# First layer's weighted sums of a two-layer graph network: lane one-hots written straight as float32r by VectorE, six of seven bins weighed by ScalarE

## What is computed

```
hi, hj = h[src], h[dst]
e = leaky_relu(concat([hi, hj]) @ w, 0.2) @ a
att = exp(e) / segment_sum(exp(e), src)[src]
out = segment_sum(hi * att, dst)
x = layernorm(x + out)
```

## Time and profile before

| | us |
|---|---|
| median of 3 runs | 3264.69 |
| lowest, highest | 3262.2, 3265.74 |
| the profiled execution: its time | 3265.05 |
| its span | 3263.3 |
| busy in the span: PE, DVE, ACT | 3041.6, 3045.0, 2752.0 |

### The profile page before, as it was taken

How to read it: one execution, slowest core, us unless ns; L and a number is a source line. 1 busy time by engine, 2 the same in 40 slices (tenths; PEclk the granted TensorE clock), 3 DMA queues, 4 the chain that set the end, 5 groups by cost and what they waited for, 6 DMA issues and landing times. The chain is left out here.

```text
span 3263.3 us, 101516 instructions
## 1 busy us (share of the span) xinstructions
PE 3041.6 (93%) x40072; PEld 2778.3 (85%) x40072; DVE 3045.0 (93%) x4921; ACT 2752.0 (84%) x6952; POOL 154.7 (5%) x251
## 2 busy tenths in 40 slices
PE   5777699999999998799999999989999999999995
PEld 4666677877777786799999999988999999999993
DVE  8999889999999999899999999989999999999996
ACT  6988788888888886899999999977888888888886
POOL 0000000000000000000000000000111111111110
PEclk9989899999999999899999999999999999999998
DMA  2000022222222222233323333324444444444431
GB/s 66 13 13 12 22 93 94 93 88 92 94 87 93 94 93 57 71 96 96 97 97 96 97 96 96 98 81 154 161 164 161 164 161 162 163 160 164 161 137 41
DMA packets 173823, 333.06 MB, mean 102 GB/s; under 512 B 54876, under 2 KB 109616, under 8 KB 173264
## 3 DMA queue, kind: packets, MB, share of 16 engines
q1 hardware_dynamic: 170996, 323.30, 30.6%
q10 hardware_dynamic: 2348, 3.20, 0.3%
HBM read 320.77 MB, written 5.66 MB: 100 GB/s over the span
## 5 line engine op out<-in xcount | busy, mean ns | idle before, releaser
L1009 PE MATMUL l_gathered<-xp,l_src_onehot 128*128 128x128 bf16 x7203 | 467.0, 221 | 11.2 <-DVE l_src_onehot L922 11.2
L1434 PE MATMUL l_gathered<-hp,l_onehot 128*128 128x128 bf16 x7203 | 458.5, 219 | 0.0
L704 PE MATMUL sc_z<-sc_onehot,pq 128*128 128x256 f32 (+1 forms) x2450 | 419.5, 293 | 23.3 <-DVE sc_leaky L617 18.3
L1009 PEld LDWEIGHTS l_gathered<-xp,l_src_onehot 128*128 128x128 bf16 x7203 | 407.9, 99 | 26.3 <-DVE l_src_onehot L922 11.7
L847 DVE TENSOR_TENSOR l_lane<-iota_b,l_lane_pairs 128x896 bf16<-128x896 bf16 x686 | 421.0, 614 | 0.0
L617 DVE SCALAR_TENSOR_TENSOR sc_leaky<-sc_z,sc_leaky 128x1024 f32<-128x1024 f32 (+3 forms) x325 | 370.1, 1139 | 53.0 <-ACT sc_leaky L788 45.7
L788 ACT ACTIVATE sc_leaky<-sc_z 128x1024 f32<-128x1024 f32 (+3 forms) x325 | 309.6, 953 | 123.6 <-PE sc_z L708 120.8
L1434 PEld LDWEIGHTS l_gathered<-hp,l_onehot 128*128 128x128 bf16 x7203 | 406.2, 98 | 0.4
L708 PE MATMUL sc_z<-sc_onehot,pq 128*128 128x256 f32 (+1 forms) x2450 | 393.8, 282 | 0.0
L1448 PE MATMUL l_acc<-e,l_lane_wide 128*128 128x132 f32 x2744 | 385.7, 283 | 0.3 <-ACT e L1512 0.3
L704 PEld LDWEIGHTS sc_z<-sc_onehot,pq 128*128 128x128 f32 x2450 | 334.4, 191 | 35.6 <-issue 34.2
(11 more groups left out here) (244 smaller groups left out, 6104.2 us busy)
## 6 DMA issues: line engine op xcount, KB each, us to landing
rows_got<-edge_rows_wide SPq DMA_DIRECT2D x338, 448.0 KB, 3.6
l_got<-edge_rows_src SPq DMA_DIRECT2D x343, 224.0 KB, 3.1
placed<-edge_rows SPq DMA_DIRECT2D x144, 512.0 KB, 3.6
out_dram<-X SPq DMA_DIRECT2D x12, 256.0 KB
S<-edge_rows_wide SPq DMA_DIRECT2D x5, 448.0 KB, 8.1
edge_rows<-e SPq DMA_DIRECT2D x98, 6.1 KB
edge_rows_wide<-e SPq DMA_DIRECT2D x98, 12.2 KB
sc_last_rows<-edge_rows SPq DMA_DIRECT2D x24, 64.0 KB, 3.4
```

The lines of the kernel that those rows point to most:

```text
L704: nc.tensor.matmul(z[:, b, 0:nw, :], PQ[:, b0 + b, q, 0:C], hot[:, r % HOTS, b, 0, 0:nw, :], start=(b == u and q == 0), stop=False)
L1009: ins = nc.tensor.matmul(gps[:, t % 2, i * P:(i + 1) * P], hot[:, t % RING, i, :], parts[:, g * GX + i, q, :], start=(q == 0), stop=(q == 2))
L1434: ins = nc.tensor.matmul(gps[:, t % 2, i * P:(i + 1) * P], dst_hot[:, t % RING, i, :], hp[:, g * GX + i, q, 0:C], start=(q == 0), stop=(q ...
```

## The change

- `find_lanes` compares the lane numbers with `k.SL` directly, each lane spread over 128 elements, and writes float32r `lane_wide` itself. There are now three buffers of it (`WIDE` = 3), and the instruction waits until tile t-3 is added up.
- `lane`, `lane_pairs`, `widen` and `stage` are gone.
- VectorE weighs one bin of a tile (the last, `LAST` = 6) with a tensor_scalar, and ScalarE the six others: `weigh_first` the four that are split, and `weigh_rest` two more, with `take_high` between them.
- take_high now waits for ScalarE's own weighing. add_up waits for weigh_rest (`messages`), for VectorE's bin (`last_message`) and for `lane_wide`.

```
@@ layer0_sums, VectorE
 def weigh(t):
     dve.wait_ge(s["gathered"], t + 1)
     if t >= 2:
-        dve.wait_ge(s["low"], t - 1)
-    nc.vector.tensor_tensor(msg[:, t % 2, 0:SPLIT], gps[:, t % 2, 0:SPLIT * P].rearrange("p (i c) -> p i c", i=SPLIT),
-                            e0[:, n, g * GX:g * GX + SPLIT].unsqueeze(2).to_broadcast([P, SPLIT, C]), ALU.mult
-                            ).then_inc(s["messages"], 1)
+        dve.wait_ge(s["added"], t - 1)
+    b = g * GX + LAST
+    nc.vector.tensor_scalar(msg[:, t % 2, LAST, :], gps[:, t % 2, LAST * P:GX * P], e0[:, n, b:b + 1], None, ALU.mult
+                            ).then_inc(s["last_message"], 1)
...
 def find_lanes(t):
-    if t >= 2:
-        dve.wait_ge(s["lane_wide"], t - 1)
-    if g == 0:
-        dve.wait_ge(s["staged"], n + 1)
-    compare_lanes(nc, k, lane[:, t % 2], lane_pairs[:, n % 2, g * GX:(g + 1) * GX, :]).then_inc(s["lane"], 1)
+    if t >= WIDE:
+        dve.wait_ge(s["added"], t - WIDE + 1)
+    nc.vector.tensor_tensor(lane_wide[:, t % WIDE], k.iota_b[:].unsqueeze(1).to_broadcast([P, GX, P]),
+                            k.SL[:, 1, n, g * GX:(g + 1) * GX].unsqueeze(2).to_broadcast([P, GX, P]), ALU.is_equal
+                            ).then_inc(s["lane_wide"], 1)
@@ TensorE
 def add_up(t):
-    pe.wait_ge(s["late_messages"], t + 1)
+    pe.wait_ge(s["messages"], t + 1)
+    pe.wait_ge(s["last_message"], t + 1)
     pe.wait_ge(s["lane_wide"], t + 1)
@@ ScalarE
-def widen(t):
-    act.wait_ge(s["lane"], t + 1)
-    if t >= 2:
-        act.wait_ge(s["added"], t - 1)
-    nc.scalar.copy(lane_wide[:, t % 2], lane[:, t % 2]).then_inc(s["lane_wide"], 1)
...
+def weigh_first(t):
+    act.wait_ge(s["gathered"], t + 1)
+    if t >= 2:
+        act.wait_ge(s["added"], t - 1)
+    weigh(t, range(SPLIT)).then_inc(s["first_messages"], 1)
+
+def weigh_rest(t):
+    act.wait_ge(s["last_message"], t + 1)
+    weigh(t, range(SPLIT, LAST)).then_inc(s["messages"], 1)
 
 def take_high(t):
-    act.wait_ge(s["messages"], t + 1)
+    act.wait_ge(s["first_messages"], t + 1)
     nc.scalar.copy(halves[:, t % 2, :, 0, :], msg[:, t % 2, 0:SPLIT]).then_inc(s["high"], 1)
...
-widen(0)
 for t in range(R):
...
-    weigh_late(t)
+    weigh_first(t)
     take_high(t)
-    if t + 1 < R:
-        widen(t + 1)
-    if t % PER == 3 and t // PER + 1 < NB:
-        stage(t // PER + 1)
+    weigh_rest(t)
```

More of the change, by code:

```diff
@@ L854, in layer0_sums @@
     R = NB * PER
-    RING, LOADS, SPLIT = 3, 4, 4
+    RING, LOADS, SPLIT, LAST, WIDE = 3, 4, 4, GX - 1, 3
     BY_SCALAR = (2, 4, 6)
@@ L866, in layer0_sums @@
             "chain", "scaled", "scaled_late", "part_high", "part_rest", "part_middle", "part_low",
-            "hot", "staged", "lane", "lane_wide", "gathered", "messages", "late_messages", "high", "low", "added", "taken", "summed", "stats")}
+            "hot", "lane_wide", "gathered", "messages", "first_messages", "last_message", "high", "low", "added", "taken", "summed", "stats")}
         loaded = [ctx.semaphore(f"l0_loaded{h}") for h in range(LOADS)]
@@ L871, in layer0_sums @@
         hot = sb("src_onehot", [P, RING, GX, P], BF16)
-        lane, lane_wide = sb("lane", [P, 2, GX, P], BF16), sb("lane_wide", [P, 2, GX, P], F32R)
-        lane_pairs = sb("lane_pairs", [P, 2, NB, 2], BF16)
+        lane_wide = sb("lane_wide", [P, WIDE, GX, P], F32R)
         msg, halves = sb("messages", [P, 2, GX, C]), sb("message_halves", [P, 2, SPLIT, 2, C], F32R)
@@ L1005, in gather @@
                         pe.wait_ge(s["messages"], t - 1)
-                        pe.wait_ge(s["late_messages"], t - 1)
+                        pe.wait_ge(s["last_message"], t - 1)
                     for i in range(GX):
@@ L1019, in add_up @@
                     for i in range(SPLIT, GX):
-                        nc.tensor.matmul(acc[:, n % 2, 0:C], lane_wide[:, t % 2, i, :].bitcast(F32), msg[:, t % 2, i, :],
+                        nc.tensor.matmul(acc[:, n % 2, 0:C], lane_wide[:, t % WIDE, i, :].bitcast(F32), msg[:, t % 2, i, :],
                                          start=(g == 0 and i == SPLIT), stop=False, skip_group_check=True)
@@ L1024, in add_up @@
                         last = g == PER - 1 and i == SPLIT - 1
-                        ins = nc.tensor.matmul(acc[:, n % 2, 0:2 * C], lane_wide[:, t % 2, i, :],
+                        ins = nc.tensor.matmul(acc[:, n % 2, 0:2 * C], lane_wide[:, t % WIDE, i, :],
                                                halves[:, t % 2, i].rearrange("p h c -> p (h c)"), start=False, stop=last,
@@ L1049, in part_middle, with weigh @@
                     nc.scalar.copy(parts[:, chunk(c), 1, :], xs[:, chunk(c), :]).then_inc(s["part_middle"], 1)
-                def widen(t):
-                    act.wait_ge(s["lane"], t + 1)
-                    if t >= 2:
-                        act.wait_ge(s["added"], t - 1)
-                    nc.scalar.copy(lane_wide[:, t % 2], lane[:, t % 2]).then_inc(s["lane_wide"], 1)
-                def weigh_late(t):
-                    n, g = divmod(t, PER)
+                def weigh(t, some):
+                    n, g = divmod(t, PER)
+                    for i in some:
+                        b = g * GX + i
+                        ins = nc.scalar.activation(msg[:, t % 2, i, :], gps[:, t % 2, i * P:(i + 1) * P], ACT.Copy,
+                                                   scale=e0[:, n, b:b + 1])
+                    return ins
+                def weigh_first(t):
                     act.wait_ge(s["gathered"], t + 1)
```

## The result

| | before | changed |
|---|---|---|
| median, us | 3264.3 (4 runs) | 3284.8 (4 runs) |
| lowest, highest | 3262.2, 3265.7 | 3284.7, 3285.8 |
| ratio, 95% interval | | 1.0062 (1.0047 to 1.0077) |
| the profiled execution's span | 3263.3 | 3283.1 |

The change makes the kernel 20.5 us slower. 3288 was forecast, in a range of 3264 to 3308.

A forecast was written before the change was run, and what follows sets the result against it. The old bound was the circle take_high, take_low, make, weigh at 2.42 us a tile; a new circle of 2.50 would replace it. From 3264.7, +27 steady, -4.5 ramp and +0.7 end gave 3288 us, range 3264 to 3308.

The forecast's parts named there:

- What bounded the kernel before: Steady tiles before: a circle of waits between ScalarE and VectorE sets 2.42 us a tile, TensorE only 0.04 behind.
- the block's extras: VectorE's L941, L946 and L950, once in 7 tiles in the old circle, 0.6 us together.
- The new circle: Gather, four bins, take_high, two bins, add_up, next gather: 5.00 us for two tiles, 2.50 a tile, +27 us.
- The alternation: Steady part: gather starts alternately 2.38 and 2.62 us apart, L1020 waiting 0.24 us once in two tiles.
- VectorE's sum hidden: VectorE's steady work with the longer compare: 2.28 us a tile, covered by TensorE's 2.38, so costing nothing.
- The 0.26 for a weighing more: ScalarE: each added bin costs 0.26 us by the L1064 row, where the skill's formula gives 0.29.
- The ramp: Start of the stage, up to gather of tile 7: shorter waits for three chunks give -4.5 us, between -6 and -1.
- The term that failed: Ramp: TensorE, at half its clock in parts, may give back some of the -5.4 us, leaving -4.5.
- The sum: Whole kernel: 27 for the steady part, -4.5 ramp, +0.7 end, +23 us in all, 3288 us.
- the circle was not short enough: Rival in the steady part: circle under 4.76 us, TensorE alone sets 2.38 a tile, 3248 us; chance 0.12.
- VectorE was not the bound: Rival in the steady part: compare over 1.22 us makes VectorE decide; at 1.5, 2.78 a tile, 3382 us; chance 0.03.
- the granted clock stayed at 1.00: Rival on TensorE's clock: a twentieth of 860 us at 1.2 GHz adds 20 us, 3308 us; chance 0.06.

The follow-up runs named there:

- Run 3: Changed kernel with ScalarE's order weigh_first, weigh_rest, take_high, so all six bins come before take_high: 3320.0 us, ratio to before 1.0166.
- Run 1: Changed kernel with add_up on TensorE summing VectorE's bin first and only then waiting for ScalarE's last two bins: 3249.8 us, ratio to before 0.9948.
- run 7: Changed kernel with ScalarE weighing all seven bins and VectorE none: 3325.1 us, ratio to before 1.0202.
- run 8: Changed kernel with VectorE weighing two bins in one tensor_tensor and ScalarE five: 3244.5 us, ratio to before 0.9940.
- run 2: Changed kernel with the compare of the lanes cut from 7 bins to 3 from the fourth tile on: 3284.1 us, ratio to before 1.0056.
- run 9: Run 1's kernel with VectorE's one bin weighed as a tensor_tensor instead of a tensor_scalar: 3247.2 us.
- run 11: Run 1's kernel and the unaltered changed kernel measured again on one chip: 3246.4 us (0.9941) and 3284.0 us (1.0054).
- run 6: Kernel before with only the new weighing (ScalarE six bins, VectorE one), bf16 compare and ScalarE's cast kept: 3482.5 us, ratio 1.0663.

## Why the prediction was right

- *What bounded the kernel before.* The circle of take_high, take_low, make and weigh at 2.34 us plus the block's extras gave 2.42. Run 3 closed the same circle once more, by another edge, and its terms added up to the measured 2.60.
- *The new circle.* Forecast 5.00 us for two tiles, measured 5.01 in the timeline and 2.50 a tile in the mean. Run 1 took a third of L1020 out of it, run 7 put a bin in and run 8 took one out, and the time moved as the sum of the circle did, until VectorE's sum was met in run 8. The alternation was there as well: in the two tiles above the gathers start 2.40 apart (1708.04 to 1710.44) and then 2.61, where 2.38 and 2.62 were forecast, and L1020 waited 171 times in the stage (forecast: about 170), for 0.18 us and not 0.24.
- *VectorE's sum hidden.* Right: the compare took 1.08 us as L904 does in the earlier trace rows, and run 2 showed that none of it is on the path. Its neighbour was mis-sized: the single bin took 0.344 us, 0.26 from start to start, where the line through the earlier trace rows gave 0.29 and 0.21. The line was right for the form that it was drawn from (0.282 in run 9), and the tensor_scalar costs 0.06 more. It didn't matter here, but it made 0.06 us a tile, 20 of the 25 us, by which the expectation of run 8 was off.
- *The 0.26 for a weighing more.* The row was right: four bins last 1.14 and two 0.62 in the changed kernel, and run 7 gives 0.26 for the seventh (5.27 - 5.01 for two tiles). By the price of the Trainium skill ("ScalarE: Activation LUTs", What ACT_TABLE_LOAD costs), 0.29 from start to start, a tile would have been 2.58 as the prediction has it, an estimate. The measurement decides for the row. By the same estimate four bins and two come to 0.18 us more than the 1.14 and 0.62 measured, where the prediction counted 0.15; that would be 2.59 a tile.
- *The ramp.* Forecast -4.5 with an end at -6, measured -6.6. The chunks went as worked out: part_rest to part_rest was 6.48, 4.30 and 6.49 us (forecast 6.4, 4.2, 6.4), in these rows of the ramp:

```profile
1308.94 1.08 DVE L909 TENSOR_TENSOR R<-R,xp 128x896 f32<-128x896 f32 x1
...
1312.31 1.08 DVE L909 TENSOR_TENSOR R<-R,xp 128x896 f32<-128x896 f32 x1
...
1318.79 1.09 DVE L909 TENSOR_TENSOR R<-R,xp 128x896 f32<-128x896 f32 x1 [1.16 <-ACT xp L1045]
...
1323.09 1.09 DVE L909 TENSOR_TENSOR R<-R,xp 128x896 f32<-128x896 f32 x1
...
1329.58 1.09 DVE L909 TENSOR_TENSOR R<-R,xp 128x896 f32<-128x896 f32 x1 [2.17 <-ACT xp L1045]
```

  From the first of these rows to the last it is 20.64 us, where before it was 25.77 (1310.40 to 1336.17): -5.1, near the -5.4 of the prediction. The term that failed is TensorE's: I let it give 0.9 us of that back. In the profiled execution it gained 1.5 us more, at the full clock in 1335 to 1340 us where the earlier trace rows has 0.75. That is partly luck. In the second profile of the changed kernel (run 11) the same three distances are 6.48, 4.31 and 6.48, but the clock was at its lower level in these 5 us, and the ramp gave 5.0 us. The two stretches, first profile and second:

```profile
1335.00:1340.00 5.00, 4.63 (x56) 4.22 (x54) 5.00 (x11) 4.14 (x14) 0.00 (x0) 1.00 0.37 88
```

```profile
1335.00:1340.00 5.00, 4.75 (x32) 4.66 (x33) 4.73 (x8) 3.30 (x9) 0.00 (x0) 0.50 0.31 82
```

- *The sum.* 27 - 4.5 + 0.7 = 23 was forecast. 26.4 - 6.6 + 0.7 = 20.5 is what the trace has for the stage. The medians differ by 20.5 too, the profiled spans by 19.8, and in run 11, on another chip, the medians by 17.8 (3284.0 and 3266.2). So the agreement to the tenth is chance; the steady part's 26.4 against 27 is what bears the forecast out.
- *The rivals.* None came: the circle was not short enough, VectorE was not the bound (run 2), and the granted clock stayed at 1.00 in 1500 to 1700 us with TensorE waiting 0.18 us every other tile.

## What to carry to other kernels

Sum each engine's work for a step, but also go around every closed path of waits, divide by the number of steps that it spans (here two, since gather(t+2) takes the PSUM buffer of tile t), and take the longest. What a third PSUM buffer would do was not run. An instruction moved to another engine can leave every sum under the bound and still be too late where it lies last in front of a wait: here 0.12 us too late a tile, and cured by letting the waiting engine begin with what was ready first. Before an instruction list is reordered, follow the waits that are there for other reasons as well; run 3 was missed by one that only keeps two engines off one PSUM bank.

## What the runs showed of the hardware

- On VectorE, weighing a 128x128 fp32 tile out of PSUM takes 0.344 us as a tensor_scalar with a column of factors (changed kernel) and 0.282 us as a tensor_tensor with the same factors broadcast (run 9); 128x256 takes 0.413 (run 8) and 128x512 0.682 (kernel before) in the second form. I had not expected the form with one tensor operand less to be the slower one.
- A compare of bf16 inputs with float32r output, 128x896, takes 1.081 us beside 0.614 with bf16 output. That is the same as a multiplication of fp32 tensors of this size (1.08). In run 7 the mean was 1.121; why was not looked into.
- TensorE's granted clock stayed at its upper level, 2.4 GHz, through the steady part (1360 to 2100 us) even in run 6, where TensorE was busy for 169 of 200 us. In the ramp it moved between the two levels, and not alike in two executions of the same kernel (1.00 and 0.50 in 1335 to 1340 us).
